# V projections of both batches in the output product's PSUM bank, and zero matmuls ahead of the score units of group 0

## What is computed

```python
h = modulated(x, cond)                     # (x * ys) @ weight, scaled by rsqrt of a sum
q, k, v = split(h @ w_qkv.T)               # 16 heads of 8, rotary embedding on q and k
scores = einsum('bhsd,bhtd->bhst', q, k) / sqrt(8)
attn = softmax(where(causal, scores, -inf))
x = x + (einsum('bhst,bhtd->bhsd', attn, v)) @ w_out.T
```

## Time and profile before

| | us |
|---|---|
| runs | 181.81, 184.06, 181.8 |
| median | 181.81 |
| profiled execution: span | 180.1 |
| PE, DVE, ACT, POOL busy | 169.0, 139.3, 134.4, 93.4 |

### The profile page before, as it was taken

The page is one execution under the profiler, slowest core; times in us unless marked ns, Lnnn a source line. Parts: engine busy times, 40 slices in busy tenths (PEclk is TensorE's granted clock), DMA queues, the critical chain, the costliest instruction groups (busy, mean ns, idle before and its releaser), DMA issues.

```text
span 180.1 us, 3258 instructions
## 1 busy us (share of the span) xinstructions
PE 169.0 (94%) x934; PEld 116.8 (65%) x934; DVE 139.3 (77%) x444; ACT 134.4 (75%) x224; POOL 93.4 (52%) x116
## 2 busy tenths in 40 slices
PE   6998989999999999988999999996999989999992
PEld 2765555765666666654648767874677867788881
DVE  5598899789898989981586998699889648637551
ACT  3569366687787788889735696953969999999970
POOL 4508188975453969696541632021769931676000
PEclk9999999999999999999999999999999999999999
DMA  4824673776666756421110799970760000001001
GB/s 132 305 46 103 179 208 118 231 257 233 177 203 187 198 181 184 157 78 49 58 55 9 217 294 361 338 229 11 234 233 0 0 4 0 0 2 58 0 4 58
DMA packets 15349, 24.28 MB, mean 135 GB/s; under 512 B 2844, under 2 KB 4828, under 8 KB 15308
## 3 DMA queue, kind: packets, MB, share of 16 engines
q1 hardware_dynamic: 14532, 23.29, 42.0%
q10 hardware_dynamic: 800, 0.79, 1.7%
HBM read 18.71 MB, written 5.27 MB: 133 GB/s over the span
## 4 chain that ended last, share of the span: by engine, by line
PE 70%; DVE 14%; ACT 8%; issue 5%; POOL 1%; ACTq 0%; DVEq 0%; POOLq 0%
PE psum L1405 11%; PE psum L1538 10%; PE psum L1466 9%; PE psum L1539 9%; PE psum L1540 9%; PE psum L1441 7%; DVE psum L772 4%; PE psum L1341 2%; PE psum L1355 2%; PE psum L1287 2%; ACT t_probs L1105 2%; PE psum L1445 2%; DVE t_raw L924 1%; PE psum L1400 1%; ACT t_q_pad L1155 1%
## 5 line engine op out<-in xcount | busy, mean ns | idle before, releaser
L772 DVE CUSTOM_DVE_ANT_0 psum<-psum,t_causal 128x128 f32<-128x128 f32 (+3 forms) x128 | 58.8, 525 | 6.0 <-PE psum L1405 3.3
L1105 ACT ACTIVATE t_probs<-psum 128x1024 f32<-128x1024 f32 (+2 forms) x48 | 40.8, 883 | 8.4 <-PE psum L1441 5.5
L1405 PE MATMUL psum<-t_stacked,t_q_pad 96*128 96x256 f32 (+2 forms) x104 | 32.1, 378 | 2.4 <-DVE t_row_max L772 1.2
L1405 PEld LDWEIGHTS psum<-t_stacked,t_q_pad 96*128 96x128 f32 x104 | 17.7, 188 | 16.3 <-DVE t_row_max L772 11.2
L672 POOL TENSOR_SCALAR_AFFINE_SELECT t_probs<-t_probs 128x512 f32<-128x512 f32 x32 | 20.5, 653 | 9.0 <-ACT t_probs L1105 8.3
L944 DVE SCALAR_TENSOR_TENSOR t_q_pad<-psum,t_zw_all,t_q_pad 128x512 fp32r<-128x512 f32 x24 | 17.8, 748 | 9.4 <-ACT t_q_pad L1153 9.3
L1139 ACT ACTIVATE psum<-psum 128x512 f32<-128x512 f32 x40 | 23.4, 586 | 1.2 <-PE psum L1540 0.6
L703 POOL TENSOR_TENSOR t_q_pad<-t_raw,t_q_pad 128x512 fp32r<-128x512 f32 x8 | 10.8, 1358 | 21.0 <-ACT t_q_pad L1155 21.0
L1466 PE MATMUL psum<-t_probs,t_v_all 128*32 128x512 f32 (+3 forms) x256 | 20.6, 439 | 0.0
L772 DVE DVE_READ_ACCUMULATOR2_ANT t_row_max<- 128x1 f32 x128 | 18.2, 142 | 0.0
L1153 ACT ACTIVATE t_q_pad<-psum,t_zw_all 128x512 fp32r<-128x512 f32 x24 | 16.5, 689 | 1.2 <-PE psum L1540 0.5
(11 more groups left out here) (232 smaller groups left out, 366.2 us busy)
## 6 DMA issues: line engine op xcount, KB each, us to landing
t_stacked<-scratch SPq DMA_DIRECT2D x16, 256.0 KB, 5.7
t_probs<-in_L_ffn_Wa SPq DMA_DIRECT2D x2, 1024.0 KB, 13.1
scratch<-t_o_sb SPq DMA_DIRECT2D x7, 256.0 KB, 2.0
t_raw<-in_experts SPq DMA_DIRECT2D x7, 256.0 KB, 3.1
t_stacked<-scratch SPq DMA_DIRECT2D x9, 192.0 KB, 2.7
t_q_pad<-scratch SPq DMA_DIRECT2D x28, 48.0 KB
scratch<-t_dn_hi SPq DMA_DIRECT2D x2, 512.0 KB, 3.2
t_q_two<-scratch SPq DMA_DIRECT2D x5, 192.0 KB, 2.6
```

The costliest lines, as they stand in the source:

```text
L772: last = V.tensor_tensor_reduce(scores, scores, causal[:, S - width:S], 1.0, 3 * BIG, ALU.add, ALU.max, row_max[s][:, qb, j:j + 1])
L1105: A.activation(o, scores, ACT.Exp, scale=float(1.0 / np.sqrt(np.float32(HD)))).then_inc(exp_done, 1)
L1405: last = T.matmul(bank[:, o:o + width], q_pad[s][0:TOP, j, qb * P:(qb + 1) * P], stacked[0:TOP, n, 0:width], start=True, stop=True)
```

## The change

V of both batches is projected into bank 6 (PV) and leaves the ring. V of batch 0 keeps its place behind max unit 6 and waits for the first selection product of Q to be placed; V of batch 1 moves behind the first laying. `copy_q0(0)` moves ahead of `copy_k0(1)`, and the counts of `rep_copied` follow. `copy_v(1)` moves to between exp(0,2) and exp(0,3), and the first output product waits for both V. PE does one matmul of 512 bf16 columns on zeros into the unit's bank, behind the wait for that bank, ahead of max units 1 to 6 and 8 to 11 of group 0. The zeros get a tile of their own, set by POOL's first memset; that of `max_pad[0]` moves behind three others.

```diff
-SLICES, LAY_AT = 11, 8
+SLICES = 11
-RING_ORDER = [("max", 0, _u) for _u in range(7)] + [("v", 0)] + [("max", 0, _u) for _u in range(7, len(MX_UNITS[0]))]
+RING_ORDER = [("max", 0, _u) for _u in range(len(MX_UNITS[0]))]
 for _n in range(GROUPS):
-    RING_ORDER += [("max", *_u) for _i in range(LAY_AT) for _u in max_units(_n, _i)]
-    RING_ORDER += [("v", 1)] if _n == 0 else []
-    RING_ORDER += [("max", *_u) for _i in range(LAY_AT, SLICES) for _u in max_units(_n, _i)]
+    RING_ORDER += [("max", *_u) for _i in range(SLICES) for _u in max_units(_n, _i)]
...
+        warm = sb("warm", [P, BANK], BF16)
...
                     if n < BY_PE:
-                        sp.wait_ge(rep_copied, 2)
+                        sp.wait_ge(rep_copied, 3)
...
-            G.memset(max_pad[0][:], 0.0).then_inc(pads_early, 1)
+            G.memset(warm[:], 0.0).then_inc(pads_early, 1)
             G.memset(f32_of(sel[:, 0, :, :]), 0.0).then_inc(sel_zero, 1)
             G.memset(dexp[:], -0.5).then_inc(exp_set, 1)
             G.memset(causal[:, 0:S - P], 0.0).then_inc(causal_zero, 1)
+            G.memset(max_pad[0][:], 0.0).then_inc(pads_early, 1)
...
                 for kb in range(KB):
                     A.copy(v_cols[:, b * NG:(b + 1) * NG, kb, :, 0:HD],
-                           ring("v", b)[:, kb * P:(kb + 1) * P].rearrange("p (g j d) -> p g j d", g=NG, j=HG)
+                           PV[:, kb * P:(kb + 1) * P].rearrange("p (g j d) -> p g j d", g=NG, j=HG)
                            ).then_inc(v_copied, 1)
...
             place_q0(3, 0)
+            copy_q0(0)
             copy_k0(1)
...
             copy_projection(0)
-            copy_q0(0)
             copy_q0(1)
...
                 exp(n, 2)
+                if n == 0:
+                    copy_v(1)
...
-                if n == 0:
-                    copy_v(1)
...
-            warm = max_pad[0][:].rearrange("p a b -> p (a b)")
-            def keep_warm(times):
+            def keep_warm(times, bank=psum[:, 0, :]):
                 for _ in range(times):
-                    T.matmul(psum[:, 0, :], warm[:, 0:P], warm, start=True, stop=True)
+                    T.matmul(bank, warm[:, 0:P], warm[:], start=True, stop=True)
...
             def project_v(b):
                 if b == 0:
                     pe.wait_ge(xc_ready[0], 1)
+                    pe.wait_ge(q0_placed, HG)
+                    pe.wait_ge(rep_copied, 2)
+                else:
+                    pe.wait_ge(v_copied, KB)
                 pe.wait_ge(xc_ready[1 + b], 1)
                 pe.wait_ge(ld_wv, 16)
-                wait_ring("v", b)
...
                     if u in (0, HG):
-                        pe.wait_ge(rep_copied, 1 + u // HG)
+                        pe.wait_ge(rep_copied, 3 if u else 1)
...
                 bank = ring("max", n, u)
+                if n == 0 and u not in (0, 7):
+                    keep_warm(1, bank)
...
                 if kb == 0 and lo == 0:
-                    pe.wait_ge(v_copied, KB * (n // NG + 1))
                     if n:
                         pe.wait_ge(pv_copied, n)
                     else:
-                        pe.wait_ge(xc_ready[2], 1)
+                        pe.wait_ge(v_copied, KB * B)
...
             lay_max_under_q(0)
+            project_v(1)
...
-                if n == 0:
-                    project_v(1)
```

More of the change, by code:

```diff
@@ L642, in place_max @@
                 else:
-                    pool.wait_ge(pads_early, n + 1)
+                    pool.wait_ge(pads_early, n + 2)
                 G.tensor_copy(max_rows[s][:, :, :, 0], row_max[s][:]).then_inc(mhi_ready, 1)
@@ L780, in place_first_max @@
                 dve.wait_ge(mx_reduced, units_to(1))
-                dve.wait_ge(pads_early, 1)
+                dve.wait_ge(pads_early, 2)
                 V.tensor_copy(max_rows[s][:, :, :, 0], row_max[s][:]).then_inc(mhi_ready, 1)
@@ L1330, in wait_ring @@
                     pe.wait_ge(mx_reduced, units_to(n, u[0] + 1))
-                elif kind == "v":
-                    pe.wait_ge(v_copied, KB * (n + 1))
                 else:
@@ L1360, in project_v @@
                     pe.wait_ge(xc_ready[0], 1)
+                    pe.wait_ge(q0_placed, HG)
+                    pe.wait_ge(rep_copied, 2)
+                else:
+                    pe.wait_ge(v_copied, KB)
                 pe.wait_ge(xc_ready[1 + b], 1)
                 pe.wait_ge(ld_wv, 16)
-                wait_ring("v", b)
                 for kb in range(KB):
-                    last = T.matmul(ring("v", b)[:, kb * P:(kb + 1) * P], xc[:, b, kb * P:(kb + 1) * P],
+                    last = T.matmul(PV[:, kb * P:(kb + 1) * P], xc[:, b, kb * P:(kb + 1) * P],
                                     w_v, start=True, stop=True)
```

## The result

The changed kernel takes 181.25 us (median of 20 runs, 180.81 to 182.0) against 181.96 us of the kernel before (20 runs); the ratio is 0.9937, 95% interval 0.9911 to 0.9964. That is 0.6% less, inside the 2% that were forecast as no change, in the stated range, and more than the 0.15 us of the forecast: 181.25 lies outside the forecast's own neighbourhood (181.4 to 181.9), between it and rival A's 181.0. Without those seven its median is 181.81, and the change is 0.56 us, 0.3%; with them its mean is 182.6 against 181.29. Of the changed kernel's 20 runs none lies there.

A forecast was written before the change was run, and what follows sets the result against it. PE was taken as the bound, 94% busy, with only group 0's end movable. Delays of 0.39 us against 1.2 us removed at 32.21 netted 0.15 us: 179.95 of span plus 1.7 around it gave 181.65 us, range 180.5 to 182.9.

The forecast's parts named there:

- the forecast's own neighbourhood: Whole kernel: 181.4 to 181.9 us around the forecast, including the case of no change; chance 0.50.
- rival A: V product at 32.21 us: its 1.2 us go almost fully, 0.84 us less, 181.0 us; chance 0.20.
- The first claim: Whole kernel: PE is a full conveyor behind 34 us, so only when PE gets through group 0 moves the end.
- The zero matmuls: Group 0's score units: 0.24 us each, mostly hidden; only unit 1 (about 0.2) and unit 11 (0.24) cost time.
- V of batch 0: Behind unit 6: product starts at 18.05 instead of 17.94 us, unit 7 comes 0.1 us later, no saving behind it.
- V of batch 1 behind the laying: Ahead of unit (1,2): costs 0.05 us, between 0.0 and 0.96; exp scores begin 0.39 us late in all.
- The late part: First exp scores to group 0's output product: the 0.39 us delay is made up, ending at 38.10 against 38.28 us.
- The forecast's 0.27 for unit (2,9): End of group 0: unit (2,9) 0.27 us early, so the output product would start at 36.57 rather than 36.85 us.
- the 1.2 us that went at 32.21: Late group 0: PE loses 0.96 us of batch 1's V product and a 0.27 us wait, 1.2 in all.
- B: POOL's work from its first select: late exp scores delay the selects, 0.1 to 0.35 us more, 182.1 us; chance 0.22.
- D, nothing happens: End of group 0: the selects end when PE arrives anyway, 181.8 us; counted within the forecast's 0.50.
- C: Clock in group 0: zero matmuls remove 184.06 us runs, median unchanged; if the other way, 184.0 us, slow side's chance 0.04.

The follow-up runs named there:

- e12_zeros_2_to_6: The changed kernel with its zero matmuls ahead of units 2 to 6 of group 0 alone; 181.18 us, ratio 0.9914.
- e7_zeros_8_to_11: The kernel before with zero matmuls ahead of units 8 to 11 of group 0 alone, V not moved; 182.2 us.
- e5_v0_only: The kernel before with batch 0's V alone moved to the output product's bank and copy_q0(0) ahead of copy_k0(1), no zero matmuls; 181.56 us, ratio 0.9961.
- e1_v_only: The changed kernel without its ten zero matmuls, both V moves kept; 181.1 us, ratio 0.991.
- e8_v_only_again: The changed kernel without its zero matmuls, measured once more; 180.95 us.
- e4_v1_only: The kernel before with batch 1's V alone moved behind the first laying, no zero matmuls; 6 of 12 runs fell, the rest 181.08 to 181.28 us.
- e10_v0_after_7: The changed kernel without zero matmuls, with batch 0's V product behind unit 7 instead of unit 6; 181.44 us.
- e9_spill_early: The changed kernel without zero matmuls, with Q of groups 2 and 3 written to DRAM ahead of SP's second K copies for group 0; 182.62 us.
- e2_zeros_only: The kernel before with the ten zero matmuls of group 0 added and V not moved; 182.35 us, ratio 0.999.

## Why the prediction was right and where it was off

*Where the gain is decided.* The first claim held: behind 38 us both kernels have the same 141.8 us, and the time moved only with the end of group 0.

*The zero matmuls.* One takes 0.23 us in the chain where PE goes straight on (0.24 forecast), and 0.35 to 0.38 where PE stood before it. VectorE got unit 1 late by 0.22 (15.06 - 14.24 against 0.60 before; 0.2 forecast). That only unit 1 and unit 11's place cost time was the forecast, and e12_zeros_2_to_6 bears it out for units 2 to 6: 0.09. The four ahead of units 8 to 11 cost 0.23 by themselves (e7_zeros_8_to_11, 23.86 less 23.63), which fits the one ahead of unit 11 alone. In all they cost 0.38 to 0.42 (0.34 forecast). The Trainium skill's sentence that weight loads overlap running matmuls only where the row groups differ ("TensorE: Matmul & The Clock Gate", Part 3, the mechanism, which excepts loads into a background buffer) does not fit: the unit behind the zero matmul at 14.55 starts as soon as it ends, 0.23 later.

*V of batch 0, the first term that failed.* The forecast left the product's own length as it was and had unit 7 0.1 us late. Alone, V's move gives 0.3 us (e5_v0_only), as project(1) ends at 7.91 instead of 8.19 from F. What was overlooked is how the wait for the bank lengthens the product: in the kernel before its first weight load begins at 17.91, behind the end of unit 6's matmul (17.84), and the product is a chain piece of 1.14 us; without the ring the loads begin under unit 6 (17.63 in e5_v0_only), the product starts 0.1 us earlier against F and takes 0.94 to 0.95. VectorE so gets unit 7 0.28 earlier, and unit 11 by the same. The other part of the step held, though its price is now known: the wait for the copies at 19.93 costs 0.05 at unit 9 and nothing behind it (0.33 against 0.28 and 0.29). Only with a zero matmul behind it does it cost something: unit 9's reduction begins 0.82 us behind unit 8's in e7_zeros_8_to_11, 0.70 in the kernel before and 0.65 in the changed one. In the changed kernel the zero matmuls hide the gain: the product starts 0.22 late against F, takes 0.89, and project(1) ends at 8.29, 0.10 late where 0.34 was forecast. The 0.25 us between 1.14 and 0.89 are that difference.

*V of batch 1 behind the laying, the second.* The forecast had the exp scores 0.39 late and they come 0.02 early. Of this miss of 0.41, 0.24 is the error above, carried on, and 0.17 is this step: 0.05 was put on the V product, and in fact the stretch from project(1)'s end to the first exp got shorter, 2.70 from 2.82. The product fills a wait that was there anyway: meanwhile VectorE reduces both (1,0) and (1,1), and PE then does (1,2) and (1,3) without a pause, four instructions from 23.94 on, 0.25 a unit in the chain, where the forecast had (1,3) wait for (1,1) and take 0.50. I had moved VectorE's reductions late by the same 0.34 and so made the product and the reductions queue behind each other.

*The late part came out right, in part by luck.* From the first exp to the end of the output product the forecast was 0.56 less (0.17 gained in spite of 0.39 late); measured 0.53 (12.62 to 12.09). So the two steps above account for the whole miss: the forecast put the end at 23.45 from F, and it is 23.08. Inside the late part two sizes were off by about 0.1 each and nearly cancelled: the product starts 0.53 nearer to the first exp, not 0.67, and loses nothing to the selects, not 0.10. The select ends at 36.38 and PE's weight loads for the second row block wait for it (36.43, 0.46 idle), but the matmuls of the first block cover that wait, and the product is 1.43 long as before. The forecast's 0.27 for unit (2,9) also doesn't follow from its own numbers, as 0.39 late and a gap of 0.49 gone leave 0.10; VectorE's row in fact closes up by 0.69 between the reductions at 32.01 and 35.49 (31.75 and 34.54 after).

*What limits the changed kernel there.* Of the 1.2 us that went at 32.21, PE gives 0.51 back: it stands before the last exp scores until POOL's spread is done (32.87), where it had work before. The forecast had these scores right behind the spread, too. POOL's row is no longer unbroken either: it idles 0.24 before 30.62, and the spread, whose row began level with the kernel before (first select 13.00 us from F, 13.03 before), ends 0.15 late.

*The rivals.* B (the delay goes through POOL) fell with the delay itself: the spread of the last queries ends 18.48 us after the first reduction, 18.33 before, so 0.15 late and not 0.39 or more. The path that B named is real, though: POOL now leads to the last exp scores. A had the right direction; V's moves alone are its 0.84 us and a little more (0.93). D, nothing happens, is out. C named the right thing: the 184 us runs are stretches at 1.2 GHz, and they are gone in the changed kernel, while the median hardly shows it. What it left out is that V's move can do it, too. Without zero matmuls and with batch 0's V out of the ring no run fell either (0 of 36 in e1_v_only, e5_v0_only and e8_v_only_again); with V in the ring and no zero matmuls 50 of 160 fell (the kernel before and e4_v1_only). Neither is a guarantee: of the two other kernels with V out of the ring and no zero matmuls, e10_v0_after_7 had two short falls in 12 and e9_spill_early 5 falls in 12, the profiled one behind a wait of 1.9 us for a DMA. The Trainium skill ("TensorE: Matmul & The Clock Gate", Part 1) has activity release the throttle and idleness restore it; the runs agree in direction, though the fall that a profile shows came with no longer wait than some tenths of a microsecond ahead of it.

*What stays open.* Why batch 0's V alone is enough is argued, not shown: the fall stood at 18.2 us, just when V's product runs, and without the ring that product starts 0.1 us earlier against F and follows unit 6 without a gap. That it is a thin margin is what e10_v0_after_7 suggests, where V comes later and two runs fell for a short time. Against work ahead of 18.2 us as the whole account stands e7_zeros_8_to_11, whose zero matmuls all come later and in which no run fell for long. Nor is it settled what spreads the changed kernel's runs over 1.2 us; the start's clock and the padded Q's landing are each seen in single profiles.

*What the zero matmuls buy.* With V's moves made, little: the two runs without them have a median of 181.04 (24 runs, no fall) against 181.25 (20 runs, no fall), and from F leaving them out saves 0.38 us. Those medians were taken at different times and were not compared with each other directly. The gain of the change is V's; alone, the zero matmuls about pay their price (mean of e2_zeros_only 182.47, of the kernel before beside it 182.55, which the interval of its ratio doesn't tell apart).

## What to carry to other kernels

A matrix product that needs a shared bank costs more than its own time: it waits for the bank, and its weight loads with it (1.14 us against 0.94 here), and its reader's copies hold the bank. Whether the copies cost anything is read from who stands behind them: 0.05 us for batch 0's, although they show as a piece of the chain. Put work that nobody waits for into a stretch in which the engine waits for another one anyway, and when you forecast that, move the other engine's work along only if it really stands behind. Look at all runs, not at the median: a clock that falls in a third of them, for 2.2 us each, is worth as much on average as the whole gain on the median, and what looks like the cure may only be one of two.

## What the hardware showed that I had not expected

The granted clock reads 1.00 in the start-up stretch, though the start-up matmuls run at half the later pace (0.45 us for 512 bf16 columns against 0.23 ahead of the score units); the later falls do show in it (0.50). A fall came behind PE's being 67 to 79% busy by the record for three microseconds, no long idle time, and lasted 6.8 us, through a stretch in which PE was fully busy; the one in e9_spill_early lasted about as long. And the same small copy can take very different times: the second K copies that were in time when issued at 19.3 us took 5.41 us when issued at 20.9 behind two larger writes (one profile; whether it is their order or the load of the queues isn't separated).
